# First attention: starting fills, row copies and rough pieces placed anew; latent weights folded in the LoRA stage; 113 contraction rows

## Chip, core and metric

The kernel runs on one core of a Trainium2 chip. The metric is the device time of one execution in microseconds. The engines are PE (TensorE, matmul), DVE (VectorE), ACT (ScalarE), POOL (GpSimd) and SP (SyncE, which here issues DMAs). They run side by side and wait for each other only through semaphores.

## What is computed

A residual stream x of 2 x 1024 tokens by 256 goes through six blocks, each behind a layer norm: a mixture of experts, an attention, the mixture again, a LoRA block with routing, a second attention with latent projections, and the LoRA block again.

```python
def _L0_attn_ref(x, Wq, Wk, Wv, Wo):           # 16 heads of 16
    scores = jnp.einsum('bthd,bshd->bhts', q, k)
    scores = scores * mask                      # masked scores are 0, not -inf
    attn = jax.nn.softmax(scores / T ** 0.5, axis=-1)
    return jnp.einsum('bhts,bshd->bthd', attn, v).reshape(B, T, H * Dh) @ Wo
...
def _L1_attn_ref(x, ...):                       # 16 heads of 128, 64 rotary
    c_q = _rmsnorm(x @ Wq_down, q_norm_w)       # latent of 48
    c_kv = _rmsnorm(x @ Wkv_down, kv_norm_w)    # latent of 64
    q, k, v = c_q @ Wq_up, c_kv @ Wk_up, c_kv @ Wv_up
    scores = (q @ k.T + q_rope @ k_rope.T) * scale
    return softmax(scores) @ v @ Wout
...
x = x + 0.5 * _L0_ffn_ref(_layernorm(x, axis=-1), ...)
x = x + _L0_attn_ref(_layernorm(x, axis=-1), ...)
x = x + 0.5 * _L0_ffn_ref(_layernorm(x, axis=-1), ...)
x = x + 0.5 * _L1_ffn_ref(_layernorm(x, axis=-1), ...)
x = x + _L1_attn_ref(_layernorm(x, axis=-1), ...)
x = x + 0.5 * _L1_ffn_ref(_layernorm(x, axis=-1), ...)
```

## The kernel before

The stages run one after the other: between two of them every engine meets at the end of a block. A stage starts with SP's `g.credit`, one increment for every semaphore that the stage uses for the first time; engines that wait for the last of them (as `s_x.at(0)` in `attention_stage`, line 664 and its like) start behind all of these. The residual g.X stays on the chip, 16 tiles of 128 tokens.

**First attention** (`attention_stage`, from line 539). Heads go in eight groups of four (NG = 8, four groups per sequence). Queries and keys of a group are projected to PSUM, split by ACT into a high part SH and by DVE into a low part SL, and laid by SP into the rows of QT and KT that one matmul contracts: per head 16 rows for each of high by high, high by low and low by high, and one row (32 or 96) with the row's maximum, which KT multiplies by -1. SP issues 24 such copies per group (line 661). QT and KT have two buffers; before the first group POOL zeroes both, sets KT's two rows to -1 and fills VV, the values with a column of ones (lines 667 to 676). ACT waits for the last of these fills before its first copy; DVE's split waits for the first three. PE's order at the start is: per token tile the transposes (line 770) and the values of the tile before (776), then both halves of the projections (795), the last values, later tiles (784, 787: masked keys count with score 0, so sums of later values are needed), then the first rough scores.

A rough score (811) is one plain matmul whose maxima DVE takes (1076): 40 pieces per group, 12 for query block 0, 28 for block 1, in two PSUM banks taken in turn, so that piece n waits until piece n - 2 is reduced. The block's maxima go through MB (`block_max`, 1085 and 1088), four transposes on PE (822) and ACT's four row copies (977) into QT. Then the exact scores (834), ACT's exponent (994), POOL's cut of later keys (696) and the values (850) follow.

The loop is written out by hand: 24 slots per group, s = 0 to 23, in each of which PE does the scores of one slot, a rough piece or more of the next group, the values of a slot before, and a filler (`filler`: tokens of the second sequence, output of the first). `per_slot` says how many rough pieces a slot has: two in each of the slots 11 to 23, and 2, 3, 2, 3, 2, 2 in slots 0 to 5, there already the group's own. The maxima of block 0 of the next group are asked for in slot 17, those of block 1 in slot 6. POOL clears the maxima rows of the next group's buffer in slot 8 (`forget_maxima`, 707), and normalises a tile of the second sequence one slot ahead of its transposes (713).

**LoRA stage** (`lora_stage`, from 1146): tiles are normalised, transposed and multiplied (1198, 1190); base products of four tiles (1208); then DVE's routing in two halves, each with one exponent on ACT (1234), and the update of x tile by tile (1223, 1311).

**Second attention** (`mla_stage`, from 1333). A block of its own loads the weights and multiplies queries into keys (1410) and values into the output (1413); ACT copies GK and UV out of PSUM (1426 to 1430) and casts high parts (WdownH, WpairH, GH), DVE takes the low parts. In the block behind, POOL zeroes QH, QL, KH and KL (1517), MB and CN, and sets KL's row 0 to -1 (1521), while DVE normalises into PT (line 140) and splits XT (1840). Heads go in pairs, eight per sequence, 16 slots each: scores are three matmuls of KH by QH, KH by QL, KL by QH over all 128 partitions (1640), rough scores one (1621). Of the rows, 113 are used: row 0 the maximum, 64 rotary, 48 latent.

## Time and profile before

| what | us |
|---|---|
| median of 3 runs | 2514.59 (2514.47 to 2517.68) |
| profiled execution, time | 2512.3 |
| its span | 2510.4 |
| first attention, from its first operation to the next stage | 348 to 842 |
| first LoRA stage | 1171.0 to 1223.2 |
| block of the latent weights | 1223.2 to 1250.8 |
| second attention | 1250.8 to 2453 |
| mean granted clock of PE, as a share of 2.4 GHz | 0.901 |

The stages' times are start times of instructions in the timeline. A row of the timeline gives start and duration in us, engine, line, operation, output and inputs; merged rows have a count (x4), and in brackets stands how long the engine had been idle and who released it. PE's matmuls overlap each other, so a row's duration is longer than its step to the next. The mark 128*64 at a PE row is rows by columns of the weights.

### The profile page before, as it was taken

The page shows a single profiled execution, that of the slowest core. Times are in us where ns is not written, and L with a number is a line of the kernel's source. Part 1 is how long each engine was busy: PE and PEld are TensorE (multiplying, and loading weights), DVE is VectorE, ACT ScalarE, POOL GpSimd, SP SyncE. Part 2 cuts the span into 40 slices and gives each one's busy share as a digit, 9 for nine tenths or more (in the row PEclk, how much of TensorE's full clock was granted, in tenths as well). Part 3 has the DMA queues.
Part 4 walks back from the last instruction along what each step waited for, and adds up shares of the span by engine and source line. Part 5 has one row for each costly group of instructions (what it writes and reads, how often), then busy time and mean ns, then how long its engine had stood idle before and what let it go on. Part 6 is the DMA issues. An engine that isn't in the chain of part 4 may idle for free. (4 is left out here: it accounts for less than half of the span.)

```text
span 2510.4 us, 32059 instructions
## 1 busy us (share of the span) xinstructions
PE 2048.8 (82%) x8868; PEld 1277.2 (51%) x8869; DVE 1252.7 (50%) x2521; ACT 794.4 (32%) x1331; POOL 867.4 (35%) x643
## 2 busy tenths in 40 slices
PE   4699708889898859982548999999976999999986
PEld 4466405545555636652434555555463555555555
DVE  4222253545565432215455666666435666666625
ACT  1122102545555312211122333333321333333322
POOL 3100171232222320006022555555600555555531
PEclk9999957989998779995757999999976999999998
DMA  7311221211120541112232222222003222222101
GB/s 315 136 59 59 67 63 28 48 26 26 26 35 17 221 182 59 59 61 71 85 57 65 51 51 50 50 50 50 5 1 76 51 53 55 55 55 54 30 1 45
DMA packets 86911, 159.83 MB, mean 64 GB/s; under 512 B 16288, under 2 KB 50592, under 8 KB 84512
## 3 DMA queue, kind: packets, MB, share of 16 engines
q1 hardware_dynamic: 64544, 127.19, 18.9%
q0 software_dynamic: 6144, 16.79, 2.0%
q10 hardware_dynamic: 16128, 14.69, 1.7%
q8 instruction: 47, 0.77, 0.1%
q14 instruction: 48, 0.39, 0.0%
HBM read 69.34 MB, written 27.39 MB: 39 GB/s over the span
## 5 line engine op out<-in xcount | busy, mean ns | idle before, releaser
L1541 POOL TENSOR_TENSOR mla_PS<-mla_PS,mla_PT 128x1024 f32<-128x1024 f32 x192 | 457.2, 2381 | 202.3 <-ACT mla_PT L1779 199.5
L1890 DVE TENSOR_REDUCE mla_MXP<-PS 128x1 f32<-128x512 f32 x512 | 342.1, 688 | 240.5 <-PE PS L1621 236.2
L1779 ACT ACTIVATE mla_PT<-PS 128x1024 f32<-128x1024 f32 x256 | 262.5, 1025 | 401.8 <-PE PS L1640 401.4
L1649 PE MATMUL PS<-mla_PT,mla_CN 128*64 128x512 f32 x1024 | 274.6, 615 | 0.4 <-ACT mla_PT L1779 0.4
L1076 DVE TENSOR_REDUCE att_MX<-PS 128x1 f32<-128x512 f32 (+3 forms) x320 | 194.4, 633 | 145.7 <-PE PS L814 116.1
L1621 PE MATMUL PS<-mla_KH,mla_QH 128*128 128x512 f32 x512 | 218.1, 465 | 33.8 <-DMA mla_KL<-mla_SL 20.5
L381 DVE COPY moe_HT<-PS 128x512 f32<-128x512 f32 x96 | 66.3, 691 | 319.8 <-PE PS L506 313.6
L1640 PE MATMUL PS<-mla_QH,mla_KH 128*128 128x512 f32 x512 | 211.0, 412 | 0.5 <-ACT mla_QH L1766 0.5
L1640 PE MATMUL PS<-mla_QL,mla_KH 128*128 128x512 f32 x512 | 202.3, 395 | 0.0
L1640 PE MATMUL PS<-mla_QH,mla_KL 128*128 128x512 f32 x512 | 201.5, 394 | 0.0
L1621 PEld LDWEIGHTS PS<-mla_KH,mla_QH 128*128 128x128 f32 x512 | 92.5, 197 | 202.9 <-DVE mla_MXP L1890 133.2
L534 POOL DMA_INDIRECT XN<-slots_out,moe_PO x32 | 32.3, 1008 | 454.9 <-DMA slots_out<-moe_YS 445.8
L994 ACT ACTIVATE att_PT<-PS 128x1024 f32<-128x1024 f32 (+1 forms) x192 | 153.3, 812 | 108.8 <-PE PS L834 105.8
L500 PE MATMUL PS<-W,moe_ST 128*128 x384 | 177.3, 605 | 2.7 <-issue 1.5
L514 PE MATMUL PS<-moe_W,moe_HT 128*128 x768 | 173.7, 379 | 0.0
L1541 POOL TENSOR_TENSOR mla_PS<-mla_PT 128x1024 f32<-128x1024 f32 x32 | 76.3, 2385 | 247.7 <-ACT mla_PT L1779 247.7
L811 PE MATMUL PS<-att_KT,att_QT 128*128 128x512 f32 (+3 forms) x384 | 144.6, 418 | 9.4 <-DVE att_MX L1076 5.7
L514 PEld LDWEIGHTS PS<-moe_W,moe_HT 128*128 128x128 f32 x768 | 142.2, 190 | 17.3
L1902 DVE RECIPROCAL PS<-PS 128x128 f32<-128x128 f32 x128 | 108.7, 917 | 79.7 <-PE PS L1656 79.7
L696 POOL TENSOR_SCALAR_AFFINE_SELECT att_PT<-att_PT 128x256 f32<-128x256 f32 x128 | 52.0, 407 | 279.2 <-ACT att_PT L994 279.1
L1640 PEld LDWEIGHTS PS<-mla_QH,mla_KH 128*128 128x128 f32 x512 | 96.6, 189 | 81.7 <-issue 35.3
L834 PE MATMUL PS<-att_QT,att_KT 128*128 128x512 f32 (+3 forms) x384 | 121.8, 410 | 0.2 <-ACT att_PT L994 0.2
(276 smaller groups left out, 3176.2 us busy)
## 6 DMA issues: line engine op xcount, KB each, us to landing
W<-in_W_dram SPq DMA_DIRECT2D x8, 2048.0 KB, 14.5
moe_W<-in_W_dram SPq DMA_DIRECT2D x8, 2048.0 KB, 35.7
moe_XS<-slots_in SPq DMA_DIRECT2D x100, 128.0 KB, 2.0
slots_out<-moe_YS ACTq DMA_DIRECT2D x96, 128.0 KB, 1.7
mla_QH<-mla_SH SPq DMA_DIRECT2D x64, 128.0 KB, 2.4
mla_KH<-mla_SH SPq DMA_DIRECT2D x64, 128.0 KB, 2.4
mla_QL<-mla_SL SPq DMA_DIRECT2D x64, 128.0 KB, 2.4
mla_KL<-mla_SL SPq DMA_DIRECT2D x64, 128.0 KB, 2.4
```

The costliest lines, as they stand in the source:

```text
L500: ins = pe.matmul(bank(2 + u)[:, :], ST[:, u, k, :], g.W1[:, experts[u], k, :], start=(k == 0), stop=(k == KD - 1))
L514: ins = pe.matmul(bank(6 + u)[:, 0:D], HT[:, u, k, :], W2[:, experts[u], k, :], start=(k == 0), stop=(k == KF - 1))
L811: ins = pe.matmul(out[:, m, :], QT[:, H % 2, h, i * P:(i + 1) * P], KT[:, H % 2, h // 2, k0:k0 + w], start=(m == 0), stop=(not diag and m ...
L834: ins = pe.matmul(st_banks(s)[:, hh, c0:HB], KT[:, G % 2, pair, j * P:(j + 1) * P], QT[:, G % 2, 2 * pair + hh, q * HB + c0:(q + 1) * HB], ...
L994: act.activation(PT[:, kk % 2, 2 * pair:2 * pair + 2, c0:HB], st_banks(s)[:, :, c0:HB], ACT.Exp, scale=SEQ ** -0.5).then_inc(s_p.handle, 1)
L1076: dve.tensor_reduce(out, bank(n % 2)[:, 0:len(hs) * w].rearrange("p (h k) -> p h k", k=w), AX_X, ALU.max).then_inc(s_mx.handle, 1)
L1541: pool.tensor_tensor(PS[:, :], PT[:, slot(0), :] if k == 1 else PS[:, :], PT[:, slot(k), :], ALU.add).then_inc(s_ps.handle, 1)
L1621: pe.matmul(bank(piece_bank(n))[:, :], QH[:, buf, h, tile * P:(tile + 1) * P], KH[:, buf, h, c * HB:(c + 1) * HB], start=True, stop=True). ...
L1640: ins = pe.matmul(bank(st_bank(s, h))[:, :], kk[:, buf, h, ks], qq[:, buf, h, qs], start=(n == 0), stop=(n == 2))
L1649: ins = pe.matmul(bank(6)[h * DKVL:(h + 1) * DKVL, :], CN[:, k, 0:DKVL], PT[:, slot(k), h * HB:(h + 1) * HB], start=(k == 0), stop=(k == T ...
L1779: act.activation(PT[:, slot(k), :], banks(st_bank(s, 0), 2)[:, :], ACT.Exp, scale=MLA_SCALE).then_inc(s_p.handle, 1)
L1890: dve.tensor_reduce(MXP[:, n // NPC, c, h, t:t + 1], bank(piece_bank(n))[:, :], AX_X, ALU.max).then_inc(s_mx.handle, 1)
```

## The change

1. First attention, start: POOL fills only MB at once, and buffer 0 of QT (0) and KT (all -1) behind the eighth normalised tile; ACT fills buffer 1 behind the second high part, and VV's columns behind the copies of the later tiles. The projections' halves start after four token tiles each; all values come after them.
2. Query and key weights are laid out so that the two heads of equal parity lie in neighbouring rows of a projection; one DMA places both, 12 instead of 24 per group.
3. Rough pieces stand in slots 8 to 23 (two each, one in 12 to 15) and 0 to 5 (two each). The block 0 maxima of the next group are taken in slot 16. DVE makes two of the four row copies, and clears the maxima rows in slots 7 and 14; POOL's `forget_maxima` is gone, and it normalises two slots ahead.
4. The weights' block of the second attention is gone: its loads, matmuls, copies and casts stand in the first LoRA stage, with the subtractions on POOL.
5. The second attention contracts 113 rows (`USED`). QH, QL, KH and KL aren't filled but for row 0, by four DMAs; ACT negates the maximum as it copies it, and KL's row 0 is +1. The stage's engines now wait for its credits.
6. The semaphores of the norms are shared by all stages (`norm_sems`).

```diff
+    FROM = 8
+    per_slot = {s: 2 for s in range(FROM, NSL)} | {s: 1 for s in range(FROM + 4, FROM + 8)} | {s: 2 for s in range(6)}
...
-                sp.wait_ge(s_fill.handle, s_fill.at(5))
+                sp.wait_ge(s_fill.handle, s_fill.at(3))
...
-                        for h in range(HG):
+                        for e in range(2):
                             for dst, at, row in rows:
...
+                                to, made = 64 * e + row, at + 2 * DH0 * e
+                                part = slice(e, HG, 2) if dst is QT else slice(0, 2)
+                                sp.dma_start(f32(dst[to:to + DH0, G % 2, part, :]), src[made:made + 2 * DH0, :]).then_inc(s_rows.handle, 16)
...
-                pool.memset(f32(QT[:, :, :, :]), 0.0).then_inc(s_fill.handle, 1)
-                pool.memset(f32(KT[:, :, :, :]), 0.0).then_inc(s_fill.handle, 1)
                 pool.memset(MB[:, :], 0.0).then_inc(s_fill.handle, 1)
...
+                pool.wait_ge(s_xn.handle, s_xn.at(TB))
+                pool.wait_ge(s_fill.handle, s_fill.at(1))
+                pool.memset(f32(QT[:, 0, :, :]), 0.0).then_inc(s_fill.handle, 1)
+                pool.memset(f32(KT[:, 0, :, :]), -1.0).then_inc(s_fill.handle, 1)
...
-                        if s == 8 and 2 <= G + 1 < NG:
-                            forget_maxima(G + 1, t)
...
-                        if (G, s + 1) in filler and filler[G, s + 1][0] == "rows":
+                        if (G, s + 2) in filler and filler[G, s + 2][0] == "rows":
...
+                for half in range(2):
+                    for t in range(4 * half, 4 * half + 4):
+                        xt_copy(t, bank(t % 2))
+                    high(0, half, bank(4 + half))
+                act.activation(QT[:, 1, :, :].rearrange("p h (n c) -> p (h n) c", c=P), ones(HG * TB), ACT.Copy, scale=0.0).then_inc(s_afill.handle, 1)
+                act.activation(KT[:, 1, :, :].rearrange("p h (n c) -> p (h n) c", c=P), ones(2 * TB), ACT.Copy, scale=-1.0).then_inc(s_afill.handle, 1)
...
+                def clear_max_rows(H, q):
+                    dve.wait_ge(s_st.handle, s_st.at(NSL * (H - 1)))
+                    dve.wait_ge(s_nm.handle, s_nm.at(8 * (H - 1)))
+                    for e in range(2):
+                        dve.memset(f32(QT[max_row(e), H % 2, e:HG:2, q * HB:(q + 1) * HB]), 0.0).then_inc(s_zero.handle, 1)
...
                         if s == 6:
                             block_max(G, 1)
+                            max_copies(G, 1)
+                        if s in (7, 14) and 2 <= G + 1 < NG:
+                            clear_max_rows(G + 1, (7, 14).index(s))
+                        if s == 16 and G + 1 < NG:
+                            block_max(G + 1, 0)
                         if s == 17 and G + 1 < NG:
-                            block_max(G + 1, 0)
+                            max_copies(G + 1, 0)
...
+                if ahead:
+                    pe.wait_ge(s_xtc.handle, s_xtc.at(NT))
+                    queries_into_keys()
+                    values_into_output(0)
+                    values_into_output(1)
+                    pe.wait_ge(ahead.s_abc.handle, ahead.s_abc.at(2))
                 mids_t(0)
...
+                    for m in range(4):
+                        act.wait_ge(ahead.s_abp.handle, ahead.s_abp.at(2 + m // 2))
+                        act.copy(ahead.UV[:, 2 * m:2 * m + 2, :].rearrange("p a d -> p (a d)"), bank(2 + m % 2)[:, :]).then_inc(ahead.s_abc.handle, 1)
                 exps(1)
...
+    USED = slice(0, 1 + RD + DQL)
...
-                for dst in (QH, QL, KH, KL):
-                    pool.memset(f32(dst[:, :, :, :]), 0.0).then_inc(s_fill.handle, 1)
```

PE, start of the first attention, from the last transposes of the first eight tiles on: before (att_XNS are normalised tokens, att_XT their transposes).

```order
L770 MATMUL PS<-C,att_XNS 128x128 x2
L776 MATMUL PS<-att_Wv,att_XT 128x256 x2
L795 MATMUL PS<-att_XT,att_Wqk 128x512 x4
L776 MATMUL PS<-att_Wv,att_XT 128x256 x2
L784 MATMUL PS<-att_VV,att_SLOW 128x256
L787 MATMUL PS<-att_VS,C 128x256
```

The same place now, from the first transposes.

```order
L760 MATMUL PS<-C,att_XNS 128x128 x8
L785 MATMUL PS<-att_XT,att_Wqk 128x512 x2
L760 MATMUL PS<-C,att_XNS 128x128 x8
L785 MATMUL PS<-att_XT,att_Wqk 128x512 x2
L766 MATMUL PS<-att_Wv,att_XT 128x256 x16
L774 MATMUL PS<-att_VV,att_SLOW 128x256
L777 MATMUL PS<-att_VS,C 128x256
```

Both halves of the projections moved ahead of all value products.

DVE in the third group, from the end of block 1's maxima (att_MB) to block 0's of the next group: before.

```order
L1088 SCALAR_TENSOR_TENSOR att_MB<-att_MX,C 128x4
L1076 TENSOR_REDUCE att_MX<-PS 128x2 x4
L1098 TENSOR_TENSOR att_F<-PS,att_F 128x256
L1099 TENSOR_TENSOR att_D<-PS,att_D 128x16
L1101 RECIPROCAL att_RC<-att_D 128x16
L1076 TENSOR_REDUCE att_MX<-PS 128x1 x8
L1085 TENSOR_SCALAR att_MB<-att_MX 128x4x4
L1076 TENSOR_REDUCE att_MX<-PS 128x1 x4
L1069 TENSOR_TENSOR att_SL<-PS,att_SH 128x512
```

The same stretch now, from the two row copies in slot 6 on.

```order
L1089 CAST att_QT<-PS 1x512 x2
L1095 MEMSET att_QT 1x2x512 x2
L1070 TENSOR_REDUCE att_MX<-PS 128x2 x4
L1070 TENSOR_REDUCE att_MX<-PS 128x1 x5
L1104 TENSOR_TENSOR att_F<-PS,att_F 128x256
L1105 TENSOR_TENSOR att_D<-PS,att_D 128x16
L1107 RECIPROCAL att_RC<-att_D 128x16
L1070 TENSOR_REDUCE att_MX<-PS 128x1
L1095 MEMSET att_QT 1x2x512 x2
L1070 TENSOR_REDUCE att_MX<-PS 128x1 x2
L1079 TENSOR_SCALAR att_MB<-att_MX 128x4x4
L1070 TENSOR_REDUCE att_MX<-PS 128x1 x2
```

Two row copies and two pairs of clears are new, the reductions (att_MX) start ahead of the sums (att_F, att_D, att_RC) in larger number, and the next maxima come ahead of their slot's pieces; two more row copies follow in slot 17.

ACT at the end of the first LoRA stage's first part: before (lora_ML are mids, lora_EX the exponents).

```order
L1238 COPY lora_ML<-PS 128x136 x2
L1234 ACTIVATE lora_EX<-lora_SH 128x64
L1253 COPY lora_MT<-PS 128x128 x16
L1164 UNCONDITIONAL_BRANCH
L1421 UNCONDITIONAL_BRANCH
L1426 COPY mla_GK<-PS 64x16x48
L1427 COPY mla_GK<-PS 64x4x48
```

The same place now.

```order
L1291 COPY lora_ML<-PS 128x136 x2
L1305 COPY mla_GK<-PS 64x16x48
L1306 COPY mla_GK<-PS 64x4x48
L1309 COPY mla_UV<-PS 128x512 x4
L1287 ACTIVATE lora_EX<-lora_SH 128x64
L1313 CAST mla_WdownH<-mla_Wdown 128x224
L1315 CAST mla_WpairH<-mla_Wpair 128x512
L1317 CAST mla_GH<-mla_GK 64x128
L1322 COPY lora_MT<-PS 128x128 x16
```

GK's and UV's copies stand ahead of the second exponent, the casts behind it.

## Rows read from the trace of the kernel before

**Rows 1.** by stretches: us, busy us (instructions) by engine, granted clock, DMA
```profile
1410.00:1600.00 190.00, 185.00 (x740) 101.51 (x739) 129.95 (x196) 73.89 (x94) 108.52 (x50) 1.00 0.22 51
```

**Rows 2.** timeline, first attention's start: start us, us, engine line op out<-in [idle<-releaser]
```profile
348.08 6.92 POOL L667 MEMSET att_QT<- 128x8192 f32 x1 [8.05 <-SPq L116]
...
351.22 7.52 DVE L140 TENSOR_SCALAR att_XNS<-X,MV,RS 128x256 f32<-128x256 f32 x2
...
373.71 0.65 ACT L957 COPY att_XT<-PS 128x256 f32<-128x256 f32 x2 [21.51 <-POOL att_VV L676]
...
376.68 0.41 DVE L140 TENSOR_SCALAR att_XNS<-X,MV,RS 128x256 f32<-128x256 f32 x1 [10.45 <-PE PS L770]
...
384.40 3.60 PE L795 MATMUL PS<-att_XT,att_Wqk 128*128 128x512 f32 x8
...
388.71 0.65 SPq L661 DMA_DIRECT2D att_QT<-att_SH  x1
```

**Rows 3.** timeline of PE, from the products with later tiles to rough scores
```profile
394.30 1.19 PE L784 MATMUL PS<-att_VV,att_SLOW 128*128 128x256 f32 x2 [5.44 <-POOL att_VS L687]
...
403.39 0.59 PE L784 MATMUL PS<-att_VV,att_SLOW 128*128 128x256 f32 x2
405.70 0.44 PE L811 MATMUL PS<-att_KT,att_QT 128*128 128x128 f32 x2 [1.71 <-DMA att_QT<-att_SL]
```

**Rows 4.** timeline of the block that multiplies the latent weights
```profile
1226.43 0.33 SPq L1398 DMA_DIRECT2D mla_WqT<-in_WqT_dram  x1
...
1238.86 3.54 PE L1410 MATMUL PS<-mla_WqT,mla_WkT 128*64 128x48 f32 x31 [16.96 <-DMA mla_Wout<-in_Wout_dram]
...
1242.30 4.18 PE L1413 MATMUL PS<-mla_Wout,mla_WvT 128*64 128x256 f32 x31
...
1246.54 2.05 ACT L1430 COPY mla_UV<-PS 128x512 f32<-128x512 f32 x4 [2.99 <-PE PS L1413]
...
1250.79 1.17 DVE L123 BATCH_NORM_AGGREGATE MV<-ST 128x2 f32<-128x6 f32 x16 [0.32 <-PEq L1393]
```

**Rows 5.** waits of PE in the first attention's loop: total us, times, longest
```profile
PE PS L864 <- ACT att_QT L977: 9.9, 4, 2.5
PE PS L776 <- ACT att_QT L977: 7.4, 3, 2.5
PE PS L770 <- POOL att_XNS L713: 7.0, 4, 3.6
PE PS L822 <- DVE att_MB L1085: 5.6, 7, 0.9
```

**Rows 6.** groups of ACT by line: xcount, busy us, mean ns, idle before
```profile
L977 ACT CAST att_QT<-PS 1x512 fp32r<-1x512 f32 x64 | 36.9, 576 | 30.1 <-PE PS L822 28.9
```

**Rows 7.** timeline of DVE, start of the program: a fill
```profile
0.92 0.27 DVE L163 MEMSET Z<- 128x256 f32 x1 [0.92 <-PEq L2078]
```

**Rows 8.** timeline of PE behind such a wait
```profile
665.26 1.77 PE L834 MATMUL PS<-att_QT,att_KT 128*128 128x512 f32 x4
```

**Rows 9.** timeline of the first LoRA stage
```profile
1177.06 4.81 DVE L140 TENSOR_SCALAR lora_XN<-X,MV,RS 128x256 f32<-128x256 f32 x7
...
1193.20 3.62 PE L1208 MATMUL PS<-lora_Wbase,lora_XT 128*128 128x256 f32 x16
...
1196.12 0.26 ACT L1234 ACTIVATE lora_EX<-lora_SH 128x64 f32<-128x64 f32 x1 [2.46 <-DVE lora_SH L1279]
```

**Rows 10.** timeline of the second attention's start
```profile
1253.04 15.61 DVE L140 TENSOR_SCALAR mla_PT<-X,MV,RS 128x256 f32 x2 [0.40 <-DVE RS L134]
...
1268.57 0.41 DVE L1840 TENSOR_TENSOR mla_XTL<-PS,mla_XTH 128x256 fp32r<-128x256 f32 x1
```

**Rows 11.** timeline of PE in a pair: 64 rows, 512 columns
```profile
1477.35 0.50 PE L1596 MATMUL PS<-mla_CTH,mla_GH 64*128 64x512 f32 x1
1477.69 0.39 PE L1596 MATMUL PS<-mla_CTL,mla_GH 64*128 64x512 f32 x1
1477.92 0.39 PE L1596 MATMUL PS<-mla_CTH,mla_GL 64*128 64x512 f32 x1
```

More of the change, by code:

```diff
@@ L53 @@
 NP1 = H1 // 2
+NLAT = DQL + DKVL
 LEAST = -3.0e38
@@ L117, in credit, with norm_sems @@
         self.fresh = []
+def norm_sems(g, turn):
+    return (g.sem("norm_" + n, each, turn) for n, each in (("stats", NT), ("deviations", 1), ("reciprocals", 1)))
 def norm_stats_dve(dve, g, s_mv):
@@ L555, in attention_stage @@
     NKEY = NSL // 2
-    NROW = 16 * 6 * HG
+    NROW = 16 * 6 * 2
     BIG = -1.0e30
@@ L575, in attention_stage @@
     NPC0 = sum(1 for p in pieces if p[0] == 0)
-    per_slot = {s: 2 for s in range(11, NSL)} | {0: 2, 1: 3, 2: 2, 3: 3, 4: 2, 5: 2}
-    assert sum(per_slot.values()) == NPC and sum(per_slot[s] for s in range(11, 17)) == NPC0
-    ordered = list(range(11, NSL)) + list(range(0, 6))
+    FROM = 8
+    per_slot = {s: 2 for s in range(FROM, NSL)} | {s: 1 for s in range(FROM + 4, FROM + 8)} | {s: 2 for s in range(6)}
+    assert sum(per_slot.values()) == NPC and sum(per_slot[s] for s in range(FROM, FROM + 8)) == NPC0
+    ordered = list(range(FROM, NSL)) + list(range(0, 6))
     begin = {s: sum(per_slot[a] for a in ordered[:n]) for n, s in enumerate(ordered)}
@@ L975, in max_copies @@
                     act.wait_ge(s_mt.handle, s_mt.at(n + 1))
-                    for h in range(HG):
+                    for h in range(2):
                         act.copy(QT[max_row(h), G % 2, h, q * HB:(q + 1) * HB], MISC[VW * h:VW * h + 1, :]).then_inc(s_nm.handle, 1)
@@ L2012, in macaron_program @@
             experts(1)
-        if "l" in stages:
-            lora_stage(nc, g, dram, 0)
-        if "L" in stages:
-            mla_stage(nc, g, dram)
+        with ExitStack() as held:
+            with ExitStack() as up:
+                latent = LatentWeights(nc, g, held, up)
+                lora_stage(nc, g, dram, 0, latent)
+            mla_stage(nc, g, dram, latent)
         if stages.count("l") > 1:
```

249 lines of the change are left out of this document (122 added, 127 removed).

## Prediction

> **What bounds the kernel now.** The profiled execution has a span of 2510.4 us and a time of 2512.3 us, 1.9 more. The runs shown have a median of 2514.6; I make the sum against 2512.3 and add the 2.3 at the end. First I read the stretches: in the second attention's pairs PE works 185 of 190 us at a granted clock of 1.00 [rows 1], so these long loops can hardly gain by order. Then the timeline of the starts of the stages, where an instruction with a long idle time before it shows who released it. Last the waits of PE in the first attention's loop.
>
> **First attention's start.** POOL zeroes QT from 348.08 on for 6.92 us, and beside it two normalisations on DVE take 7.52 together, where a later one takes 0.41. More fills follow, and ACT makes its first copy at 373.71, released by the last of them. The projections run at 384.4, SP starts its 24 row copies at 388.71 [rows 2]. PE's products with the later tiles last from 394.30 to 404.0, and the first rough score starts at 405.70, released by a row copy's landing [rows 3].
>
> The row says 7.52 us for two operations beside a fill of 6.92. The Trainium skill's page "SBUF — State Buffer", section "Who interferes with whom", has a lock on the ports that DVE and GpSimd share, in which the second one waits out the whole instruction of the first; by that rule, the trace agrees.
>
> After the change the first eight normalisations have no fill beside them but a small one. I take 352.7 for PE's first transpose (an estimate: the third weight DMA is issued at 349). Four tiles take 2.5 us; half a projection, 4 records, takes 1.8 at the high clock, where 8 took 3.60 [rows 2], and 3.6 at the low one. So the second half of the projections is in PSUM at about 365. Behind the eighth normalisation, at 361, POOL fills half of QT (half of 6.92) and half of KT (1.7 by the same rate), to 366.2. SP waits for these and starts 22 us earlier than before; its twelve issues by 0.65 and a landing of 2 us bring the rows at 376. They are no longer last. ACT now fills the other halves before it copies values: 512 elements take 0.51 [rows 4], so 4096 and 2048 take 6.1, to 371. Only then are values copied: six of the eight value tiles by 1.0 to 1.7 each, to 379.5; POOL's six adds take 4.8 as before, to 384.3; PE's products 9.7 as before [rows 3], to 394.0. **-11.7** for the first rough score. Then 28 instead of 26 pieces stand ahead of the loop, but they leave the loop: 0. DVE makes two of the four row copies there and waits for the transposes ahead of them: +1.5. **Term A: -10.2.** Bounds: -17 (values and products at the high clock), -4 (fills and values 6 us later).
>
> **First attention's loop,** eight groups of some 50 us. PE waits for ACT's row copies 2.5 us at a time, seven times shown; for POOL's normalised rows 7.0 in all; for the first block's maxima 5.6 [rows 5]. The wait for the second block's maxima stays. A row copy takes 0.58 on ACT [rows 6]; DVE takes two of the four, so seven waits shrink by 1.1: -7.7. The first block's maxima are asked for a slot earlier, after four slots with one piece instead of two: -5.6. Normalising comes a slot earlier and POOL has no clears ahead of it: -6.4 of 7.0. Against that, in slot 17 DVE waits for the transposes and copies two rows, 1.3 us; two pieces fewer in slots 0 to 5 give 1.3 back: 0. The clears are now DVE's: a fill of 256 elements takes 0.27 there [rows 7], so 1024 take 1.1 and four of them 4.3 per group, in slots 7 and 14. Slot 7 has no pieces and slot 14 one: hidden behind scores and values of PE; with that cover gone six groups lose 26. The row copies fall from 24 to 12 issues per group, 15.6 to 7.8 us of SP, so that rows land 10 us into a group, about slot 5, and pieces can start in slot 8 instead of 11: nobody waits. **Term B: -19.7.** Bounds: +6 (26 - 19.7), and -36: behind each long wait PE is at the low level of its clock (1.2 GHz), where four score records take 1.77 [rows 8], and I put a kept clock at 2 us per group, 8 x 2.
>
> **The fold into the LoRA stage.** Before, the stage ends at 1223.2 and the second attention's first DVE operation is at 1250.79 [rows 4]: 27.6 us, in which SP's semaphore credits take 3.2, loading 12.4, multiplying and copying the rest. In the LoRA stage the loads stand behind its own four and land before they are wanted, and PE has room behind the base products, which end at 1196.8 [rows 9]. But ACT's exponent of the second half, on which DVE's routing waits, is queued behind GK and UV. Keys by queries took 3.54 at the low clock [rows 4], I take 2.2: 1199.3. ACT copies GK, 1.1. Half of values by output takes 1.3 (16 of 31 records in 4.18 would be 2.1 at the low clock), two UV copies 0.51 each; the second half waits for these, then two more. The exponent ends near 1204.8 instead of 1196.4 [rows 9]: +8.4, six more credits in it. POOL's three subtractions, 2.3 us, fall on the routing; beside POOL's adds seven normalisations took 4.81 [rows 9], 0.28 each more than alone: +0.5. The second attention now starts with 36 credits, 2.5 us for which all engines wait. Its first DVE operation: 1223.2 + 8.9 + 0.3 + 2.5 = 1234.9 instead of 1250.8, **-15.9**.
>
> [...]
>
> **The second attention's start.** Two normalisations take 15.61 beside POOL's fills of QH, QL, KH and KL, and the first low part of XT comes at 1268.57 [rows 10], 17.8 after the first operation. Without fills: 2.25 to the reciprocal, 0.4, transposes 0.7, ACT's copy and hand-over 0.6: 3.95. **-13.8.** The four row DMAs that take the fills' place are wanted 50 us later: 0. **Term C: -29.7.** Bounds: -33 (products at the high clock), -25 (low clock throughout, the lock in full).
>
> **113 rows.** Matmuls on 64 rows start 0.23 us apart (1477.69, 1477.92), the first after a change of form 0.34 before its successor [rows 11]; those on 128 rows have the same 0.23. So fewer rows save nothing. Whether 113 beside 128 is a change of form no row shows: 0 to +0.1 at some 8 changes in each of 16 pairs, +13. I take 0, since 113 is nearer to 128 than 64 is. The minus sign in ACT's copy: 0.
>
> **Sum:** 2512.3 - 10.2 - 19.7 - 29.7 = 2452.7; with 2.3 for the median, **2455.0**.
>
> **Rivals.** (1) The loop gives nothing: DVE's clears, its copies and its wait in slot 17 eat what PE's shorter waits bring. For it: DVE holds all maxima and is asked for more. Against: slots 7 and 14 have few pieces. 2474.7. (2) More: PE keeps its clock through shortened waits and the starts run at the high level; all terms at their low bounds, 2514.6 - 86 = 2428.6. Against: 1.4 us of wait stay. (3) The fold is paid back in the LoRA stage, exponent 13 us later with cold products (C -25), and A at its bound of -4: 2465.9. (4) Slower: a weight load of 113 rows isn't taken ahead under the running matmul. Place: the 2048 rough and score matmuls of the second attention (4 x 512). It decides from 60 / 2048 = 29 ns each; a step of 0.34 as behind a change of form [rows 11], 0.11 more, costs 225 us: 2680. Against: with 64 rows the step stays 0.23. (5) The change doesn't spread the pieces as it says, since they wait in slot 8 for rows: 2 us in seven groups and no gain of B, 2489.
>
> **How the numbers follow.** Forecast 50%, rival 1 18%, rival 2 11%, rival 3 14%, rival 4 4%, rival 5 3%. The range for 8 in 10 goes from 2434, between rival 2 and the forecast, to 2480, which holds rivals 1 and 3. All but rival 4 end faster by more than 0.2% (5 us, about what a measurement of this kernel can tell from no change): faster 0.95, same 0.01, slower 0.04.
>
> **What would show it.** The first rough score 12 us earlier and released by the products ahead of it; waits for row copies of 1.4; no normalisation on DVE over 1 us; the LoRA stage 9 us longer and no block behind it; 0.23 at 113 rows. I am wrong if a group still takes 50 us, if PE waits for DVE in slots 14 to 17, or if steps at 113 rows exceed 0.25.

## The result, and the profile of the changed kernel

The changed kernel takes 2458.84 us (median of 4 runs, 2449.08 to 2460.5) against 2514.53 before: the ratio is 0.9769, with a 95% interval of 0.9741 to 0.9797. The prediction was 2455.0. The profiled execution took 2460.4 us, its span is 2458.5, 51.9 less than that of before. Each of the two kernels has one profile here, so a difference of a few us in one stretch can be chance; how much is shown below, at the run of the changed kernel again.

Where it went, by stage. A stage is taken from the start of its first DVE operation (the aggregation of the norm's statistics) to that of the next; the first attention is cut at its first exact score, the second at its first rough score. The last column is the sum's.

| stretch | before | after | difference | predicted |
|---|---|---|---|---|
| first mixture | 348.1 | 349.4 | +1.3 | 0 |
| first attention, to the first exact score | 79.1 | 66.3 | -12.8 | -10.2 |
| first attention, loop and end | 417.1 | 396.5 | -20.6 | -19.7 |
| second mixture | 326.8 | 326.9 | +0.1 | 0 |
| first LoRA stage with the latent weights | 79.8 | 67.7 | -12.1 | -15.9 |
| second attention, to the first rough score | 72.7 | 60.0 | -12.7 | -13.8 |
| second attention, the rest | 1130.5 | 1132.9 | +2.4 | 0 |
| second LoRA stage, store | 56.4 | 58.8 | +2.4 | 0 |

**The second attention's pairs.** The stretch of the changed kernel that answers to [rows 1] (the same columns: PE, PEld, DVE, ACT, POOL busy, granted clock, DMA):

```profile
1365.00:1555.00 190.00, 184.97 (x742) 102.47 (x740) 128.96 (x193) 71.98 (x91) 108.79 (x51) 1.00 0.22 51
```

PE is busy 184.97 of 190 us at the full clock, as before: nothing was won or lost there.

**The first attention's start**, timeline of all engines but PE, which answers to [rows 2]:

```profile
352.61 0.73 DVE L146 TENSOR_SCALAR att_XNS<-X,MV,RS 128x256 f32<-128x256 f32 x2
...
362.13 3.51 POOL L679 MEMSET att_QT<- 128x4096 f32 x1 [12.45 <-DVE att_XNS L146]
...
365.59 3.62 ACT L1014 ACTIVATE att_QT<-C 128x4096 fp32r<-128x4096 f32 x1
367.41 0.73 SPq L670 DMA_DIRECT2D att_QT<-att_SH  x1
...
369.11 1.90 ACT L1015 ACTIVATE att_KT<-C 128x2048 fp32r<-128x2048 f32 x1
...
379.82 3.93 POOL L691 TENSOR_TENSOR att_VS<-att_VS,att_VV 128x256 f32<-128x256 f32 x5
```

The first two normalisations now take 0.73 together instead of 7.52, SP starts at 367.41 instead of 388.71, and ACT's two fills (L1014, L1015) stand ahead of its value copies. PE from the sums of later values on, which answers to [rows 3]:

```profile
371.32 7.13 PE L766 MATMUL PS<-att_Wv,att_XT 128*128 128x256 f32 x24 [4.53 <-ACT att_VV L951]
383.89 1.19 PE L774 MATMUL PS<-att_VV,att_SLOW 128*128 128x256 f32 x2 [5.44 <-POOL att_VS L691]
...
392.70 0.52 PE L801 MATMUL PS<-att_KT,att_QT 128*128 128x128 f32 x2
...
415.74 1.06 PE L824 MATMUL PS<-att_QT,att_KT 128*128 128x512 f32 x2
```

PE waits 4.53 us for a value copy and 5.44 for POOL's adds. The first rough score, at 392.70, waits for nothing: no longer for the rows' landing. It stands 43.3 us behind the stage's first operation instead of 57.7.

**The first attention's loop**, waits of PE (total us, times, longest), which answers to [rows 5]:

```profile
PE PS L812 <- DVE att_MB L1082: 11.9, 8, 1.5
PE PS L801 <- DVE att_MX L1070: 8.4, 25, 0.8
PE PS L856 <- DVE att_QT L1089: 6.0, 4, 1.5
PE PS L766 <- DVE att_QT L1089: 4.5, 3, 1.5
PE PS L801 <- DMA att_QT<-att_SL: 1.8, 1, 1.8
PE PS L774 <- DVE att_QT L1089: 1.5, 1, 1.5
PE PS L801 <- issue: 1.1, 2, 0.6
```

The waits for row copies are 1.5 each instead of 2.5, those for block 0's maxima (5.6) and for POOL's normalised tiles (7.0) are gone. New are 1.8 for rows and 1.1 without a releaser, and the wait for single maxima grew from 5.0 to 8.4.

**The first LoRA stage**, PE, ACT and DVE around the latent weights, which answers to [rows 9] and [rows 4]:

```profile
1164.51 3.62 PE L1239 MATMUL PS<-lora_Wbase,lora_XT 128*128 128x256 f32 x16
...
1165.71 0.23 DVE L1348 TENSOR_TENSOR lora_SH<-lora_LG,lora_MX 128x64 f32<-128x64 f32 x1
...
1168.05 2.01 PE L1253 MATMUL PS<-mla_WqT,mla_WkT 128*64 128x48 f32 x31
...
1173.13 1.95 PE L1261 MATMUL PS<-mla_Wout,mla_WvT 128*64 128x256 f32 x16 [1.27 <-ACT mla_UV L1309]
...
1176.08 0.27 ACT L1287 ACTIVATE lora_EX<-lora_SH 128x64 f32<-128x64 f32 x1
...
1176.45 0.22 DVE L1350 TENSOR_REDUCE lora_SM<-lora_EX 128x8 f32<-128x64 f32 x1 [10.51 <-ACT lora_EX L1287]
...
1176.94 0.49 DVE L1352 TENSOR_TENSOR lora_PB<-lora_EX,lora_RC 128x64 f32<-128x64 f32 x1
```

DVE hands over the shifted logits (L1348) at 1165.94, and ACT makes their exponent at 1176.08, behind all copies of GK and UV: DVE stands for 10.51 us. The product at 1176.94 (L1352) matters further down.

**The second attention's start**, which answers to [rows 10]:

```profile
1206.77 1.17 DVE L129 BATCH_NORM_AGGREGATE MV<-ST 128x2 f32<-128x6 f32 x16 [2.40 <-SPq L117]
...
1210.30 0.73 DVE L146 TENSOR_SCALAR mla_PT<-X,MV,RS 128x256 f32 x2 [0.40 <-DVE RS L140]
...
1211.90 0.42 DVE L1872 TENSOR_TENSOR mla_XTL<-PS,mla_XTH 128x256 fp32r<-128x256 f32 x1 [0.86 <-ACT mla_XTH L1764]
```

Two normalisations take 0.73 instead of 15.61, and the first low part of XT comes 5.13 us after the stage's first operation instead of 17.78.

### The profile page after: what moved, and what is told of

The parts are those of the page before. It is cut to its first block and busy times, and to the rows that moved or that the text cites. A ratio compares the mean times of both kernels' runs of the same rounds, so it can differ in the third digit from the quotient of the medians.

```text
span 2458.5 us, 31965 instructions
## 1 busy us (share of the span) xinstructions
PE 2048.2 (83%) x8868; PEld 1280.4 (52%) x8869; DVE 1271.3 (52%) x2574; ACT 785.9 (32%) x1303; POOL 811.5 (33%) x625
## 5 line engine op out<-in xcount | busy, mean ns | idle before, releaser
L1651 PE MATMUL PS<-mla_KH,mla_QH 113*128 113x512 f32 x512 | 218.1, 466 | 34.3 <-DMA mla_KL<-mla_SL 21.0
L1670 PE MATMUL PS<-mla_QH,mla_KH 113*128 113x512 f32 x512 | 211.4, 413 | 0.6 <-ACT mla_QH L1797 0.6
L1670 PE MATMUL PS<-mla_QL,mla_KH 113*128 113x512 f32 x512 | 202.3, 395 | 0.0
L1670 PE MATMUL PS<-mla_QH,mla_KL 113*128 113x512 f32 x512 | 201.5, 394 | 0.0
L1651 PEld LDWEIGHTS PS<-mla_KH,mla_QH 113*128 113x128 f32 x512 | 92.5, 196 | 203.5 <-DVE mla_MXP L1922 133.2
L1670 PEld LDWEIGHTS PS<-mla_QH,mla_KH 113*128 113x128 f32 x512 | 96.6, 189 | 81.9 <-issue 35.4
```

Source lines behind the costliest of these rows:

```text
L1651: pe.matmul(bank(piece_bank(n))[:, :], QH[USED, buf, h, tile * P:(tile + 1) * P], KH[USED, buf, h, c * HB:(c + 1) * HB], start=True, stop= ...
L1670: ins = pe.matmul(bank(st_bank(s, h))[:, :], kk[USED, buf, h, ks], qq[USED, buf, h, qs], start=(n == 0), stop=(n == 2))
```

## The experiments

The kernels ran in three groups, each on one chip beside the kernel before. Where a term is smaller than the scatter of the runs, it is read from the stage it belongs to, cut as in the table above.

### The changed kernel again

> The changed kernel itself, unaltered, beside the kernel before and three variants on one chip. Its four runs so far lie between 2449.1 and 2460.5, and the first attention's loop, the same code in two profiles, took 396.5 and 391.6 us. If the loop's time varies with PE's granted clock from run to run, this profile shows a third value between some 390 and 398 with the same instructions, and the median lies between 2453 and 2460. If the difference of 5 us came from something in the variant, it shows 396 to 397 again.

Measured: 2459.32 us (5 runs, 2456.05 to 2460.27), ratio to before 0.9779 (0.9765 to 0.9792). Its profile has 396.5 us for the loop, 66.2 for the start, 67.7 and 60.0 for the two other stretches that changed. So the profile repeats itself, and by the expectation's own test that speaks for something in the other run: 391.6 us was the loop of the run with the fold undone (below). But that run's edit touches neither the loop nor anything ahead of it. In the eight profiles in which the loop is unaltered it took 396.5 (three times), 396.4, 395.8, 391.6, 390.0 and 387.2 us; the last is the profile of the fastest of five runs. The changed kernel's own nine runs hold one that may be like these: 2449.08 us, at a mean granted clock of 0.911 over the whole execution, the others at 0.907 to 0.911 and 2456 or more. The two ends, the changed kernel and the last one of this section, each over its own loop (columns as above):

```profile
415.70:812.20 396.50, 357.32 (x2031) 219.45 (x2029) 257.80 (x465) 200.80 (x308) 88.07 (x190) 0.94 0.22 29
```
```profile
403.20:790.40 387.20, 350.57 (x2031) 213.63 (x2029) 257.78 (x466) 200.45 (x308) 87.79 (x190) 0.96 0.22 29
```

The counts differ by one record, DVE and ACT are busy equally long, and PE is busy 357.32 us at a mean granted clock of 0.94 in the one, 350.57 at 0.96 in the other. What moves is PE's clock; what sets it off in one run and not in another stays open. A single profile's loop is therefore known to some 5 us only (up to 9 between the two ends), and a claim on the loop below rests on its waits too. The loop of before has two profiles, 417.1 and 418.6 us.

### 113 rows alone

```diff
-    QH[:, buf, h, ...], KH[:, buf, h, ...]
+    QH[USED, buf, h, ...], KH[USED, buf, h, ...]
```

> The kernel before with one edit: the second attention's rough and exact scores contract rows 0 to 112 instead of all 128; the fills and everything else stay as they were. By the sum's term (fewer rows save nothing and cost nothing) 2514.5 us, no change, and 0.23 us from one 512-column matmul to the next. By its upper bound (a change of form some 8 times in each of 16 pairs) up to +13, 2527. By rival 4 (the load of 113-row weights is not taken ahead under the running matmul, 0.11 us each) +225, 2740.

Measured: 2516.58 us (10 runs) against 2515.58 (13 runs), ratio 1.0002 (0.9992 to 1.0012). Timeline of PE, a rough score and exact scores on 113 rows:

```profile
1481.95 0.39 PE L1641 MATMUL PS<-mla_QH,mla_KH 113*128 113x512 f32 x1
1482.18 0.40 PE L1641 MATMUL PS<-mla_QL,mla_KH 113*128 113x512 f32 x1
1482.42 0.39 PE L1641 MATMUL PS<-mla_QH,mla_KL 113*128 113x512 f32 x1
```

The step is 0.23 us as with 128 rows. Rival 4 and the bound of +13 fall; fewer rows change the time by no more than the interval holds, -2.0 to +3.0 us.

### Row copies all on ACT

```diff
-                    for h in range(2):
+                    for h in range(HG):
                         act.copy(QT[max_row(h), ...], MISC[...])
...
-                max_copies(0, 0)      # and its two like in slots 6 and 17, on DVE
```

> The changed kernel with one part undone: ACT makes all four row copies of a block's maxima again, DVE none. The step says that PE's waits for the copies grow from 1.5 to 2.5 us each at the middle of the eight groups, 7 to 8 us in all, so 2458.8 + 7.7 = 2466.5, and up to 2 us per group more if PE's clock falls with the longer wait (2482). The rival, that DVE's copies only move the wait to the maxima that queue behind them (waits for maxima went from 5.0 to 8.4 us), expects PE's waits for att_MX back at 5 us, a net of 4 us and 2463. By rival 1 (nothing gained in the loop) 2459.

Measured: 2456.91 us (2455.57 to 2459.91), ratio 0.9767 (0.975 to 0.9783); the loop took 396.7 us. Waits of PE in the loop:

```profile
PE PS L856 <- ACT att_QT L967: 9.9, 4, 2.5
PE PS L766 <- ACT att_QT L967: 7.4, 3, 2.5
PE PS L801 <- DVE att_MX L1070: 5.3, 18, 0.8
PE PS L774 <- ACT att_QT L967: 2.5, 1, 2.5
```

The waits for copies are back at 2.5 each, 19.8 instead of 12.0 in all, but those for maxima fell from 8.4 to 5.3 and the new 1.8 and 1.1 are gone. Of 7.8 us, 6.0 had only changed their name, and the loop's time shows nothing of the remaining 1.8. The start, where DVE's two copies stand ahead of the loop, took 64.5 us; in the six profiles in which nothing of it was altered it took 65.0 to 66.8. The step worth 7.7 in the sum brought nothing that can be measured.

### Pieces in the old slots

```diff
-    FROM = 8
+    FROM = 11
-    per_slot = {s: 2 for s in range(FROM, NSL)} | {s: 1 for s in range(FROM + 4, FROM + 8)} | {s: 2 for s in range(6)}
+    per_slot = {s: 2 for s in range(FROM, NSL)} | {0: 2, 1: 3, 2: 2, 3: 3, 4: 2, 5: 2}
...
-                        if s == 16 and G + 1 < NG:
+                        if s == 17 and G + 1 < NG:
                             block_max(G + 1, 0)
```

> The changed kernel with one part undone: rough pieces stand in slots 11 to 23 and 0 to 5 as before (two each, three in slots 1 and 3), 26 ahead of the loop, and the maxima of block 0 are asked for in slot 17 instead of 16; DVE's copies and clears, the twelve wide row DMAs and the starts stay. The step says that PE's wait for block 0's maxima comes back, 5.6 us, and 2464.4; if the evener pieces also hold PE's clock (its busy time in the stage fell by 5.1 us with the same instructions) up to 2470. If the spread is worth nothing, 2459. Since DVE then asks for the maxima and waits for PE's transposes in one slot, a little more than 5.6 may show.

Measured: 2469.16 us (2468.28 to 2471.4), ratio 0.9814 (0.9797 to 0.983), 10 above the changed kernel; the loop took 410.0, 13.5 more. Waits of PE in the loop:

```profile
PE PS L801 <- DVE att_MX L1070: 14.3, 25, 1.9
...
PE PS L812 <- DVE att_MB L1079: 5.7, 7, 0.9
```

The 5.7 for block 0's maxima are back as expected, and besides them the wait for single maxima is 14.3 instead of 8.4. The even spread is worth both, 11.6 us less 2.9 for the waits that it brings (rows, and those without a releaser), 8.7 in all. Of the rest of the 13.5, 3.3 is PE's busy time, 360.62 instead of 357.32 us. Part of this is only moved: with the old slots 26 pieces stand ahead of the loop instead of 28, and the start took 64.0 us instead of 66.3. With DVE's copies and clears in the kernel, the spread is worth the 10 us of the time, about half of the loop's gain.

### Normalising one slot ahead

```diff
-                        if (G, s + 2) in filler and filler[G, s + 2][0] == "rows":
+                        if (G, s + 1) in filler and filler[G, s + 1][0] == "rows":
```

> The changed kernel with one part undone: POOL normalises a tile of the second sequence one slot ahead of its transposes instead of two. Before the change PE waited 7.0 us in four places for these tiles. If the slot was what helped, most of it comes back, 5 us or more, 2464 to 2466. If it was that POOL no longer clears the maxima rows ahead of them (3.66 us for two clears in the trace of before), at most 1 us comes back: 2459.

Measured: 2460.17 us (2455.83 to 2461.57), ratio 0.9782 (0.9767 to 0.9798); loop 396.5. The waits of PE in the loop have one row more than those of the changed kernel:

```profile
PE PS L760 <- POOL att_XNS L705: 1.0, 2, 0.5
```

1.0 us comes back, not 7.0. So it was not the slot; what is left by elimination is the clears that POOL no longer makes. No run puts them back.

### Narrow row copies

```diff
-    NROW = 16 * 6 * 2
+    NROW = 16 * 6 * HG
...
-                        for e in range(2):
+                        for h in range(HG):
...
-                                sp.dma_start(f32(dst[..., part, :]), src[made:made + 2 * DH0, :])
+                                sp.dma_start(f32(dst[..., part, :]), src[made + h // 2:made + 2 * DH0:2, :])
```

> The changed kernel with 24 row copies of 16 rows per group instead of 12 of 32 rows; the bytes, the weights' layout and everything else stay. In the traces a narrow copy lands 2.3 us after its issue, a wide one 4.6 to 7.1 us after. SP is busy 15.6 instead of 7.8 us per group. If the step of the sum is right that nobody waits for rows any longer, nothing moves: 2459. If the count of issues was what delayed the rows, they land later than 8 slots into the group and PE waits at piece 0 of each group for 2 to 5 us: 2475. If the slow landing of wide copies cancels the saved issues, the one wait of 1.8 us in group 1 stays about as it is and the first rows land near 385 instead of 382, hidden behind the later values.

Measured: 2458.96 us (2456.15 to 2464.09), ratio 0.9787 (0.977 to 0.9804). The issues of the last copies of a group (count, KB each, median us from issue to landing), wide in the changed kernel, then narrow:

```profile
att_QT<-att_SL SPq DMA_DIRECT2D x16, 128.0 KB, 7.1
```
```profile
att_QT<-att_SL SPq DMA_DIRECT2D x32, 64.0 KB, 2.3
```

The medians hide an order. The first and the last of the twelve wide copies of group 0 in the changed kernel, issued at 367.41 and 374.55:

```profile
att_QT<-att_SH SPq DMA_DIRECT2D x1, 128.0 KB, 3.5
```
```profile
att_QT<-att_SL SPq DMA_DIRECT2D x1, 128.0 KB, 7.4
```

SP issues a wide copy every 0.65 us, and they land about 1.0 us apart, so each waits a little longer than the one before. The narrow ones, issued at the same pace, all land within 2.2 to 2.3 us. From the first issue to the last landing that makes 14.5 us for twelve wide copies and 16.9 for 24 narrow ones: halving the issues gave 2.4 us of the 7.6 that SP saves. PE waits for rows once in either kernel, 1.8 and 4.1 us, at piece 0 of group 1. So the third outcome of the expectation holds nearly, and nobody but group 1 waited for either.

### The fills of the first attention back on POOL

```diff
-                pool.memset(MB[:, :], 0.0)
-                pool.wait_ge(s_xn.handle, s_xn.at(TB))
-                pool.memset(f32(QT[:, 0, :, :]), 0.0)
-                pool.memset(f32(KT[:, 0, :, :]), -1.0)
+                pool.memset(f32(QT[:, :, :, :]), 0.0)
+                pool.memset(f32(KT[:, :, :, :]), -1.0)
+                pool.memset(MB[:, :], 0.0)
+                pool.memset(VV[:, :, :], 0.0)      # then its columns of ones; ACT's four fills gone
```

> The changed kernel with the first attention's fills back on POOL at the stage's start (both buffers of QT and KT whole, MB, VV and its column of ones, some 15 us in a row), ACT's four fills gone; the order of projections and values, the wide row copies and all behind stay as changed. If POOL's fills hold DVE's normalisations as the 7.52 us for two of them say, the eighth normalised tile comes 5 to 8 us later than 362, and against that ACT saves 5.4 us ahead of the value copies: the first exact score 1 to 4 us later than in the changed kernel, 2461. If fills on POOL hold nobody and only their order on ACT and POOL mattered, the saving on ACT shows alone: 4.5 us earlier, 2454.

Measured: the time is 2458.26 us (2456.71 to 2461.73), ratio 0.9784 (0.9769 to 0.9799), no difference to the changed kernel. In its profile the attention's start took 71.3 us instead of 66.3, and the loop 390.0, at a higher mean clock. Timeline of the start:

```profile
348.98 6.92 POOL L674 MEMSET att_QT<- 128x8192 f32 x1 [7.92 <-SPq L117]
...
352.13 7.52 DVE L146 TENSOR_SCALAR att_XNS<-X,MV,RS 128x256 f32<-128x256 f32 x2
355.85 3.66 POOL L675 MEMSET att_KT<- 128x4096 f32 x1
...
359.74 7.06 POOL L677 MEMSET att_VV<- 128x8192 f32 x1
...
360.06 7.51 DVE L146 TENSOR_SCALAR att_XNS<-X,MV,RS 128x256 f32<-128x256 f32 x2
...
377.21 0.73 SPq L668 DMA_DIRECT2D att_QT<-att_SH  x1
```

The four first normalisations of DVE stand behind these fills, 7.5 us for each two: of the first two, one comes out as QT's fill ends and one as KT's does (PE takes them up at 356.20 and 359.71), the next two behind VV's fill (367.10). The rows start at 377.21 instead of 367.41. The first of the two readings is right, with a start 5.0 us longer where 1 to 4 were expected. That the time did not follow stays open: the profile has the loop shorter by 6.5, with PE's clock as the only thing that differs, and one profile cannot say whether all four runs did the same.

### The fold undone

The latent weights go to a block of their own behind the LoRA stage, as in the kernel before.

> The changed kernel with one part undone: the first LoRA stage is without the latent weights, and a block of its own between it and the second attention loads and multiplies them as before (DVE takes the low parts); the second attention's start stays without POOL's fills. The traces of before and after give 79.8 and 67.7 us from the LoRA stage's first operation to the second attention's: +12.1, 2470.9. The sum's term was 15.9, 2474.7. If the fold gives nothing beside the missing fills, 2459.

Measured: 2464.68 us (2459.97 to 2470.25), ratio 0.9796 (0.9776 to 0.9815). The stretch from the LoRA stage to the second attention took 78.3 us, 10.6 more than in the changed kernel; its loop of the first attention took 391.6 in that profile, 4.9 less, which fits a time only 5 us longer. The fold is worth the 10.6 of its own stretch. The exponent of the second half:

```profile
1156.23 0.26 ACT L1287 ACTIVATE lora_EX<-lora_SH 128x64 f32<-128x64 f32 x1 [2.47 <-DVE lora_SH L1348]
```

It comes 24.9 us after the stage's first operation at 1131.29, against 37.0 in the changed kernel.

### The second attention's fills back on POOL

```diff
                 pool.wait_ge(s_x.handle, s_x.at(0))
+                for dst in (QH, QL, KH, KL):
+                    pool.memset(f32(dst[:, :, :, :]), 0.0)
```

> The changed kernel with one thing put back: POOL zeroes QH, QL, KH and KL (4 x 3.5 us) at the start of the second attention, and SP's four row DMAs wait for it. Nobody wants these tiles before the rough scores 50 us later. If the fills hold DVE's two normalisations as in the kernel before (15.61 us for two), the first rough score of the second attention comes 12 to 14 us later than in the changed kernel: 2458.8 + 12.7 = 2471.5, by the sum's term 2472.6. If the old delay was that DVE had to wait for the tiles themselves and not the port, nothing moves: 2459.

Measured: 2465.79 us (2459.07 to 2469.76), ratio 0.9799 (0.9781 to 0.9816). The first rough score comes 69.0 us after the stage's first operation instead of 60.0: 9.0 later. Timeline:

```profile
1207.07 3.52 POOL L1550 MEMSET mla_QH<- 128x4096 f32 x1 [27.96 <-SPq L117]
...
1210.57 10.65 DVE L146 TENSOR_SCALAR mla_PT<-X,MV,RS 128x256 f32 x2 [0.40 <-DVE RS L140]
...
1217.42 3.66 POOL L1550 MEMSET mla_KL<- 128x4096 f32 x1
...
1217.68 0.69 PE L1591 MATMUL PS<-C,mla_PT 128*128 128x128 f32 x2 [14.37 <-DVE mla_PT L146]
...
1221.28 0.69 PE L1591 MATMUL PS<-C,mla_PT 128*128 128x128 f32 x2 [2.91 <-DVE mla_PT L146]
```

PE gets its first normalised tile as the third fill ends, and the second as the fourth does, 1221.28. The tiles that are filled are wanted by nobody there: it is the fill that holds DVE. Before, a fifth fill of 3.5 us (KL's row 0) followed, and the two tiles came out one fill later each, with the fourth (PE at 1265.11) and the fifth (1268.71): that is the difference to 12.7.

### The exponent first

```diff
                 mids_copy(NT - 1)
+                exps(1)
                 if ahead:
...
-                for t in range(NR):
-                    base(t)
...
                     values_into_output(0)
+                for t in range(NR):
+                    base(t)
+                if ahead:
                     values_into_output(1)
```

> The changed kernel with two moves in the first LoRA stage: ACT makes the exponent of the second half before it copies GK and UV, and PE does the base products between the two halves of values by output, where it waited 1.3 us for ACT. DVE stood 10.5 us for that exponent. The routing then ends near 1171.6 of the changed kernel's time instead of 1181.7, PE's first LoRA output near 1176.5 is the next thing in the way: the updates start 5 us earlier, 2453.8. If DVE's wait was the whole delay, 10 us and 2449. If PE's products were the bound all along, 1.3 us and 2457.5.

Measured: 2450.49 us (2440.32 to 2452.63), ratio 0.9733 (0.9711 to 0.9755), 9 below the changed kernel; the stretch took 61.6 us, 6.1 less. Timeline, the exponent and the first update of x:

```profile
1164.28 0.26 ACT L1287 ACTIVATE lora_EX<-lora_SH 128x64 f32<-128x64 f32 x1 [1.10 <-DVE lora_SH L1348]
...
1175.25 0.42 DVE L1380 SCALAR_TENSOR_TENSOR X<-PS,X 128x256 f32<-128x256 f32 x1 [5.70 <-PE PS L1276]
```

The exponent follows its input at once. The update, 5.70 us of idle before it, now waits for PE, whose second half of values by output (from 1170.18 on) stands ahead: DVE's wait moved to PE's products, as expected. The stretch accounts for 6.1 of the 9 us; which of the two moves brought how much of it no run separates.

### Rough pieces first

PE does block 0's pieces right behind the values, and the sums of later values between block 1's; ACT copies values ahead of its fills.

> The changed kernel with the first attention's start in another order: ACT copies the values before it fills buffer 1 of QT and KT, PE does block 0's twelve rough pieces right behind the values, while POOL adds later values (PE stood 5.4 us there) and then the sums of later values between block 1's first sixteen pieces, each of which waits for a maximum anyway; the sums go to PSUM banks 2 and 3. Rows have landed at 377 us, the values end near 373 without the wait for ACT's fills (4.5 us), so that the first exact score comes near 402 instead of 415.7: 2458.8 - 13 = 2446. If DVE's maxima, 28 at 0.7 us, set the pace whatever stands between them, 378 + 12 x 0.62 + 3 + 16 x 0.8 = 401, the same. If ACT, which has fills, copies and sums to carry in this stretch, is late, the gain is 5 us: 2454.

Measured: 2448.3 us (2444.04 to 2453.0), ratio 0.9736 (0.9718 to 0.9755); the start took 57.1 us, 9.2 less (13 were expected). The first rough score:

```profile
382.36 0.66 PE L801 MATMUL PS<-att_KT,att_QT 128*128 128x128 f32 x2 [10.13 <-DMA att_QT<-att_SL]
```

PE stands 10.13 us for the rows. They land at 382.36, not at 377 as I had taken; the twelve wide copies queue behind each other, which the later values hid in the changed kernel and which is the bound here. PE also comes out of that wait at the low level of its clock: the granted clock was 0.50 in the five us ahead of the first rough score.

### Both, with half of the sums ahead

> The changed kernel with the two moves in the first LoRA stage (exponent of the second half ahead of the copies of GK and UV, base products between the halves of values by output) and a new order in the first attention's start: values are copied ahead of ACT's fills, four sums of later values stand where PE waited 10 us for the rows to land, then block 0's twelve rough pieces, then each other sum with four pieces of block 1. The two parts gave 8.8 and 11 us alone. The sums taken out of the last stretch give 2.5 us more: 2459 - 8.8 - 11 - 2.5 = 2436.7. If DVE's maxima set that last stretch, 2439. If PE at a low clock does the four sums more slowly than the rows land, 2441.

Measured: 2437.15 us (5 runs, 2430.13 to 2442.78), ratio to before 0.97 (0.9681 to 0.9719). By the two ratios to before that is 0.8% below the changed kernel (0.97 against 0.9779, with intervals that lie apart), and the fastest kernel of this study. The start took 55.4 us and the LoRA stretch 61.9.

## Why the prediction held, step by step

The time lay 3.8 us above the forecast, and each of the four stretches with a term came out within 4 us of it. Their sum is -58.2 for -59.6. From profile to profile the forecast was 2452.7 and the time 2460.4; most of these 7.7 us lie in the stretches without a term. The steps inside the terms did not all hold, and in two of the terms the sum came out by luck.

**Start of the first attention, -12.8 for -10.2.** Point by point: SP's first row copy at 367.41 (predicted near 366.7), POOL's adds from 379.02, just ahead of the 379.5, the first rough score at 392.70 for 394.0, in a stage that began 1.4 later than before. The sums of later values took 8.8 us instead of 9.7, since PE's clock rose earlier. One step was wrong and had no price: the rows were to land at 376, on a landing of 2 us, and landed near 382 (as the run with rough pieces first shows). The 10 us of cover that the later values gave is why the sum did not notice; that was luck. The 28 pieces ahead of the loop for 26, put at 0, and DVE's two copies there, put at 1.5, came to 2.3 and 1.8 us by the two runs that undo them; an unaltered start varies by nearly as much, 65.0 to 66.8. And [rows 2] shows only one of the fills: the second of the two normalisations in 7.52 us waited out the fill of KT behind it (354.94, 3.66 us), not QT's. The fills hold DVE without any semaphore between them, so the engines of this kernel do not wait for each other only through semaphores.

**Loop, -20.6 for -19.7.** Right in sum, wrong in its parts: that the sum fits is luck. PE's waits of over 1 us in all, by line, add up to 49.2 us before (beside [rows 5], 11.8 for block 1's maxima, 5.0 for single ones and 2.5 for one more row copy), and to 35.2 in the rows of after. Of the 20.6 that is 14.0; the other 6.6 is PE itself, busy 363.8 us before and 357.3 after, which no step had (two of its pieces now stand ahead of the loop, and the mean granted clock is 0.94 for 0.93). The step on the row copies (-7.7) failed: it priced the copy that ACT no longer makes, and not the maxima that queue behind DVE's copy; the run with all copies on ACT takes 396.7 us for the loop. The step on block 0's maxima (-5.6) held for that wait, but the same spread also keeps single maxima from waiting, and with the old slots 13.5 us came back. The step on the normalised tiles (-6.4) held; of its two causes it was not the slot, which leaves the clears. The clears stayed hidden, at 0.91 us each, four per group, for the 1.1 worked out from [rows 7]; a row copy takes DVE 0.69, where it took ACT 0.58 [rows 6]. The group of the clears on DVE (count, busy us, mean ns, idle before):

```profile
L1095 DVE MEMSET att_QT<- 1x1024 f32 x24 | 21.9, 912 | 6.4 <-issue 6.4
```

Rival 5 was there in one group, 1.8 us. One sign of being wrong was badly set: a group was not to take 50 us any longer, and it takes 49.6 in the mean, where it took 52.1 before.

**The fold, -12.1 for -15.9.** The stage got longer by 13.1 us up to its last DVE operation, not by 8.9. The exponent stands 37.0 us behind the stage's first operation, 11.9 later than before, where I had 8.4. Of the missing 3.5, the bias that DVE waits for came 1.9 later: SP issued its load 0.8 later, behind more credits, and it was used 4.5 us after its issue instead of 3.3, now with the loads of the latent weights issued right behind it (that these delay it is argued, not shown). PE's products up to the base took 1.4 longer, partly at the low clock (records of four in 1.11 where most take 0.63). PE's latent products and ACT's copies themselves went as worked out: 8.2 us from the base's end to the exponent's, for 8.0. Behind the exponent, the routing took 5.17 instead of 4.92 us, 0.25 for POOL's subtractions where 0.5 was taken. The bound of term C had the lock in full here; no run shows that. All of the 0.25 is in one instruction, the product L1352: it took 0.49 instead of 0.22 us and came out at 1177.43, as POOL's first subtraction ended (1176.69, 0.66 us); the maximum and index searches beside the other two subtractions took what they took before. In the run with the exponent first no subtraction stands beside the product, and it takes 0.23, the routing 4.92. The Trainium skill's page "SBUF — State Buffer", section "Who interferes with whom", lets a DVE instruction with two inputs in SBUF contend with one on POOL that reads SBUF, and one with a single input outside the two-port modes not at all; the trace agrees. The update of the first tiles met a PE at the low clock, another 1.0.

**The second attention's start, -12.7 for -13.8,** went as worked out. The first low part of XT came at 5.13 for 3.95, since ACT, which now waits for the credits, loads its function table 1.25 us behind the stage's first operation (1208.02), and before beside it (1250.76). **113 rows:** 0, shown by a run of its own.

**Rivals.** Rival 1 (loop gives nothing) and 5 fell with the loop's time; 2 (more, the clock kept) by 30 us, though one run of the changed kernel comes down to 2449; 3 was half true: the fold was paid back by 4 us more than I had, and A did not sit at its bound; 4 fell with the 0.23. The 6.1 us in stretches that the change doesn't touch (the first mixture, the second LoRA stage, the rest of the second attention) are not explained. The rest of the second attention took 1134.0 with 113 rows alone and 1131.7 to 1134.7 in the variants, so that 1130.5 before may be the lucky one of two: of the 3.5 us between before and 113 rows alone, 2.7 are PE's busy time (1052.95 and 1055.61) and the waits agree within 1 us. That 113 rows cost a little of this is not excluded; the second LoRA stage took 56.4 and 56.5 in the two profiles of before and its relative, 56.5 to 59.2 in those of the variants, and I have no mechanism for it.

## What to carry to other kernels

An operation that is given to a second engine is worth what the waits behind it leave over: look who is queued there before its duration is counted. Where work is folded into another stage, the short instruction on which a chain hangs must stand ahead of the long copies; here one line, and the base products moved with it, were worth 6 us. A fill on POOL that nobody waits for can still hold DVE; put it where DVE is idle, or on ACT. Fewer, larger copies help only until they queue behind each other: look at the landing of the last of them, not at the count of issues.

## What the runs showed of the hardware

Twelve row copies of 32 partitions (128 KB each as the profile counts), issued 0.65 us apart, land 3.5 us after their issue at the first and 7.4 at the last, about 1.0 us apart; copies of 16 partitions and half the bytes, issued at the same pace, all land after 2.2 to 2.3. A normalisation that DVE starts beside fills on POOL comes out as a fill ends, and not always the first to end: with four fills in a row, the one started at 1210.57 came out behind 1217.48, past the end of one at 1214.04; in the kernel before, the first tile came out with the fourth fill's end. Adds and subtractions of POOL hold DVE less than fills do: in the changed kernel, beside adds of 0.74 us each, fifteen normalisations in the first LoRA stage took 10.70 us (0.71 each, where two with nothing beside them take 0.73 together), and beside three subtractions only one product of the routing took longer, 0.49 us for 0.22. The same loop, with equal instructions, takes between 387 and 397 us as PE's granted clock is 0.96 or 0.94 in the mean, and that is more than several of the effects that were looked for.
